# Decoder layer on one core: probabilities turned by TensorE instead of by DMA, routing moved to GpSimd, keys quantised in PSUM

## What is computed

```python
x = x + attn(layernorm(x))                 # each token's 16 heads against each other's channels, RoPE
x = x + cross(layernorm(x), ctx)           # 16 heads of 16, 2048 queries x 2048 keys
x = x + moe(layernorm(x))                  # 8 experts, top 2, and a shared expert
# cross: q, k rounded to 127 levels per head and token, v per channel,
#   p = softmax(q k^T);  s = max(p)/255;  p = round(p/s)*s;  out = (p v) Wp + bp
# moe:   g = sigmoid(x Wg); the two largest of g + bias keep g, the others get 0
#   out = sum_e silu((g_e x) w1_e) * ((g_e x) w3_e) @ w2_e + shared(x)
```

## Time and profile before

| | |
|---|---|
| median of 3 runs (range) | 1097.98 us (1095.16 to 1098.07) |
| profiled execution, its own time | 1099.65 us |
| span of the profiled execution | 1097.9 us |
| granted PE clock, mean | 0.899 of full |
| busy: PE, DVE, ACT, POOL | 71%, 88%, 70%, 64% of the span |
| DMA queue of SP | 76% of the 16 engines' span |
| first `keep_scores` starts | at 115.82 us |
| last exponential ends | at about 1062.1 us |

### The profile page before, as it was taken

The page is one execution under the profiler, slowest core; times in us unless marked ns, Lnnn a source line. Parts: engine busy times, 40 slices in busy tenths (PEclk is TensorE's granted clock), DMA queues, the critical chain, the costliest instruction groups (busy, mean ns, idle before and its releaser), DMA issues. The chain is left out here.

```text
span 1097.9 us, 21898 instructions
## 1 busy us (share of the span) xinstructions
PE 777.0 (71%) x7206; PEld 463.3 (42%) x7328; DVE 967.4 (88%) x1907; ACT 768.0 (70%) x1019; POOL 704.1 (64%) x776
## 2 busy tenths in 40 slices
PE   6766655767686867777686858686767867776764
PEld 4434333444343534444344534443434444444443
DVE  4895888999999999999998999999999999898952
ACT  2434666688777777776868877777778686878762
POOL 6445886867676768768686768686776858620101
PEclk9876688989999999889998999899899889899986
DMA  6011478979796979798896969697979789699970
GB/s 220 1 39 43 84 136 143 167 123 166 129 161 123 172 121 172 128 140 159 137 180 116 169 116 173 120 178 121 164 134 154 145 136 178 118 160 148 172 130 5
DMA packets 540887, 147.71 MB, mean 135 GB/s; under 512 B 534115, under 2 KB 538726, under 8 KB 540390
## 3 DMA queue, kind: packets, MB, share of 16 engines
q1 hardware_dynamic: 540774, 146.31, 76.0%
HBM read 9.96 MB, written 2.10 MB: 11 GB/s over the span
## 5 line engine op out<-in xcount | busy, mean ns | idle before, releaser
L1066 DVE TENSOR_SCALAR_CACHE_REDUCE score<-ps_score,q_neg 128x1024 f32<-128x1024 f32 x512 | 636.7, 1276 | 39.9 <-PE ps_score L1408 38.2
L757 ACT ACTIVATE prob<-score,exp_bias 128x2048 uint16<-128x2048 f32 x256 | 511.6, 1999 | 50.9 <-DVE exp_bias L1076 50.5
L1408 PE MATMUL ps_score<-keys,queries 128*128 128x512 bf16 x902 | 304.6, 413 | 135.3 <-DVE score L1066 116.7
L1426 PE MATMUL ps_pv<-prob_t,values 128*32 128x128 f16 x4096 | 152.0, 233 | 53.6 <-DMA prob_t<-prob 53.3
L508 POOL TENSOR_TENSOR product<-hs_exp,v_tok 128x1024 f32<-128x1024 f32 x64 | 149.1, 2353 | 47.7 <-ACT hs_exp L725 47.7
L1426 PEld LDWEIGHTS ps_pv<-prob_t,values 128*32 128x32 f16 x4096 | 128.8, 103 | 115.0 <-issue 115.0
L518 POOL TENSOR_TENSOR folded<-product 128x512 f32<-128x512 f32 x128 | 165.5, 1315 | 10.7 <-DVE hs L1003 7.0
L1408 PEld LDWEIGHTS ps_score<-keys,queries 128*128 128x128 bf16 x1024 | 70.2, 101 | 237.4 <-DVE score L1066 195.7
L508 POOL TENSOR_TENSOR product<-qk_rot 128x1024 f32<-128x1024 f32 x64 | 149.4, 2357 | 4.0 <-POOL qk_rot L501 4.0
L799 ACT ACTIVATE routed_both<-normed,routed_gate 128x256 bf16<-128x256 f32 x124 | 52.7, 496 | 94.2 <-POOL routed_gate L484 94.2
L1280 PE MATMUL ps<-routed_both,w 128*128 128x128 bf16 x512 | 47.2, 248 | 17.8 <-ACT routed_both L806 16.9
(11 more groups left out here) (133 smaller groups left out, 1225.9 us busy)
## 6 DMA issues: line engine op xcount, KB each, us to landing
prob_t<-prob SPq DMA_TRANSPOSE x256, 4.5
prob_t<-in_w SPq DMA_DIRECT2D x3, 1024.0 KB, 5.0
x_in<-in_x SPq DMA_DIRECT2D x16, 128.0 KB, 3.3
score<-in_cond_t SPq DMA_DIRECT2D x4, 512.0 KB, 6.9
out<-x_out SPq DMA_DIRECT2D x16, 128.0 KB, 2.5
w_qkv<-in_w_qkv SPq DMA_DIRECT2D x1, 768.0 KB, 4.3
early<-in_w_kv SPq DMA_DIRECT2D x1, 512.0 KB
w_s<-in_w_s SPq DMA_DIRECT2D x3, 128.0 KB
```

The lines of the kernel that those rows point to most:

```text
L757: act.activation(prob[:, s, :].bitcast(U16), score[:, s, :], ACT.Exp, bias=exp_bias[:, s:s + 1], scale=-1.0, accum_out=prob_sum[:, t.par, ...
L1066: dve.tensor_scalar(score[:, s, HALF * i:HALF * i + HALF], ps_score[:, i].rearrange("p b k -> p (b k)"), q_neg[:, t.par, h:h + 1], None, A ...
L1408: mm = pe.matmul(ps_score[:, i, b, :], queries[:, t.par, h // 2, h % 2, :], keys[:, h // 2, k0:k0 + KEYS], start=True, stop=True)
L1426: mm = pe.matmul(out[j], beside_zeros(values, i, h + j), prob_t[:, (h + j) % RING, i, :], start=(i == 0 and first), stop=(i == T - 1 and l ...
```

## The change

- The turning of the probabilities goes from the DMA to PE: `turn(h)` makes 16 transposes into a slot of `ps_score`, two substeps after the head's scores (`TURN = 2`), and a 128x1024 copy as int32 (`keep_turned`) brings them to SBUF. ACT makes 12 of a tile's 16 copies, DVE the four at substeps 11 to 14.
- The two slots of `ps_score` now serve three users in a fixed round: half 0, half 1, the turned probabilities of head `h-2`.
- The sigmoid moves from DVE to POOL (`choose` has 13 operations, one of them a power). PE spreads the gates along the partitions (`spread_gates`, 4 fp32 matmuls of 128 columns, twice), ACT keeps them (`keep_gates`, 128x512, twice), and POOL multiplies the tokens that are already turned by them (`route`, 128x1024, twice), ahead of `shift_scores`. ACT's `route` and `keep_routed` and PE's `routed_turn` are gone.
- POOL folds the value products once more (4 `fold_more` of 128x256 a tile), and DVE reduces two halves at once: 2 + 2 reductions of 512 numbers a tile in place of 4 of 256 and 4 of 512.
- Two of the small results of the query rounding stay in PSUM and one operation goes.
- Keys: all intermediate results stay in PSUM, in three banks by turns; values use one bank. The first two tiles' own values and projection use other banks, and the order of the first stage is changed to fit (queries of the first tile are turned after two of the four value turns; `cast_experts(1)` comes after the queries).
- Last tile: DVE chooses the experts (`choose_last`, 7 operations with a sort of 8) and multiplies by the gates straight from PSUM (`route_last`), and `experts_out` begins after four experts.

```diff
-                        sp.dma_start_transpose(prob_t[:, h % RING], prob[:, h % RING, :]
-                                               ).then_inc(prob_turned[h % RING], 16)
...
+TURN = 2
+DVE_KEEPS = (11, 12, 13, 14)
+        def key_bank(u):
+            return ps_score[:, u % 3 // 2, u % 3 % 2, :]
+        def slot(h, i):
+            return (h + i) % 2
...
             def scores(h, i, t):
-                if (due := t.due(2 * H, 2 * h + i - 1)) is not None:
+                if (due := t.due(2 * H, 2 * h + (0 if i == 0 else -1))) is not None:
                     pe.wait_ge(score_kept, due)
+                if i == 1 and (due := t.due(H, h - TURN)) is not None:
+                    pe.wait_ge(turn_kept, due)
...
-                    mm = pe.matmul(ps_score[:, i, b, :], queries[:, t.par, h // 2, h % 2, :],
+                    mm = pe.matmul(ps_score[:, slot(h, i), b, :], queries[:, t.par, h // 2, h % 2, :],
...
+            def turn(h, t):
+                pe.wait_ge(prob_ready, t.count(H, h + 1))
+                pe.wait_ge(score_kept, min(t.count(2 * H, 2 * (h + TURN) + 1), T * 2 * H))
+                if (due := t.due(H, h - 1)) is not None:
+                    pe.wait_ge(turn_kept, due)
+                out = ps_score[:, slot(h + TURN, 2)].rearrange("p b k -> p (b k)").bitcast(F16)
+                for i in range(T):
+                    mm = pe.transpose(out[:, P * i:P * i + P], prob[:, h % RING, P * i:P * i + P], ident_f16[:])
+                mm.then_inc(turn_made, 1)
...
+            def keep_turned(h, t):                       # ACT; DVE has the same with tensor_copy
+                act.wait_ge(turn_made, t.count(H, h + 1))
...
+                act.copy(prob_t[:, h % RING].rearrange("p k q -> p (k q)").bitcast(I32),
+                         ps_score[:, slot(h + TURN, 2)].rearrange("p b k -> p (b k)").bitcast(I32)
+                         ).then_inc(turn_kept, 1)
...
+            def route(i, t):                             # POOL
+                pool.wait_ge(gate_kept, t.count(2, i + 1))
...
+                pool.tensor_tensor(routed_t[:, EG * i:EG * i + EG],
+                                   normed_t[:, 2].unsqueeze(1).to_broadcast([P, EG, C, P]),
+                                   gate_wide[:, EG * i:EG * i + EG, :].unsqueeze(2).to_broadcast([P, EG, C, P]),
+                                   ALU.mult).then_inc(routed_kept, 1)
...
                     if n.exists() and h == 13 + late:
                         keep_queries(n)
+                    if m.exists() and t.exists() and h in (13, 14):
+                        keep_gates(h - 13, m)
                     if a.exists() and h == 14:
                         head_exp(a)
+                    if h >= TURN and t.exists() and h not in DVE_KEEPS:
+                        keep_turned(h - TURN, t)
...
-                dve.tensor_tensor(k_int[:], kp, over(k_inv[:], HD), ALU.mult).then_inc(k_chain, 1)
+                dve.tensor_tensor(kp, kp, over(k_inv[:], HD), ALU.mult).then_inc(k_chain, 1)
```

More of the change, by code:

```diff
@@ L230, in layer_kernel @@
         bank = {n: ctx.enter_context(nc.psum_tensor(f"ps_{n}", [P, 512], F32)) for n in (5, 6, 7)}
+        q_max = bank[5][:, 0:H]
+        q_float = heads(bank[6][:, D:2 * D])
+        k_max = bank[7][:, 0:2 * H]
         bank_bf = {n: bank[n][:, :].bitcast(BF16) for n in bank}
@@ L262, in layer_kernel @@
         prob_ready = sem("prob_ready")
-        prob_turned = [sem(f"prob_turned{i}") for i in range(RING)]
+        turn_made = sem("turn_made")
+        turn_kept = sem("turn_kept")
         pv_done = sem("pv_done")
@@ L586, in body @@
                     fold_more(3, a)
+                if m.exists() and t.exists():
+                    route(0, m)
+                    route(1, m)
                 if a.exists():
@@ L607, in _ @@
             all_scores(first)
+            ln_scale(0, second)
             shift_scores(first)
@@ L612, in _ @@
             fold(G + 1, first)
-            ln_scale(0, second)
+            fold_more(G, first)
+            fold_more(G + 1, first)
             value_products(2, first)
@@ L617, in _ @@
             fold(G + 3, first)
+            fold_more(G + 2, first)
+            fold_more(G + 3, first)
             norm_ho(first)
[L620 to L621 removed]
             rope(second)
@@ L630, in _ @@
             fold(G + 1, second)
+            fold_more(G, second)
+            fold_more(G + 1, second)
             over_tiles(body)
@@ L771, in keep_one @@
                     act.wait_ge(xo_projected, due)
-                act.copy(x_one[:, t.par, :], bank[7][:, 0:D]).then_inc(one_done, 1)
+                act.copy(x_one[:, t.par, :], one_bank(t)[:, 0:D]).then_inc(one_done, 1)
             def keep_two(t):
@@ L1045, in quantise_queries @@
+                dve.wait_ge(q_chain, t.count(5, 2))
+                dve.reciprocal(q_inv[:], q_neg[:, t.par, :]).then_inc(q_chain, 1)
+                dve.wait_ge(q_chain, t.count(5, 3))
+                dve.scalar_tensor_tensor(out=q_float, in0=heads(bank[6][:, 0:D]), scalar=-HD ** -0.5,
                                          in1=over(q_inv[:], HD), op0=ALU.mult, op1=ALU.mult).then_inc(q_chain, 1)
-                dve.wait_ge(q_chain, t.count(6, 5))
+                dve.wait_ge(q_chain, t.count(5, 4))
@@ L1470, in routed_turn @@
                 for e in range(EG):
-                    for c in range(C):
-                        j = C * e + c
-                        mm = pe.transpose(bank_bf[6 + i][:, P * j:P * j + P],
-                                          routed[:, EG * i + e, P * c:P * c + P], ident_bf[:])
-                mm.then_inc(routed_turned, 1)
+                    mm = pe.matmul(bank[6 + i][:, P * e:P * e + P], routed_gate[:, EG * i + e:EG * i + e + 1]
+                                   .to_broadcast([P, P]), ident[:], start=True, stop=True)
+                mm.then_inc(gate_spread, 1)
             def experts(i, j, t):
```

413 lines of the change are left out of this document (220 added, 193 removed).

## The result

The changed kernel takes 1221.32 us (median of 4 runs, 1220.84 to 1221.92) where the kernel before, on the same chip, takes 1097.05 (1095.16 to 1098.07). The ratio is 1.1135, with a 95% interval of 1.1116 to 1.1154: 124 us slower. The forecast was 1167, in a range of 1065 to 1205. The direction was right, the size was not, and the time is almost that of rival C, 1225. Whether it is C's mechanism as well is what most of the experiments ask.

What follows compares the result with a forecast made beforehand. The prediction took DVE, 88% busy, to set the tiles. From a span of 1097.9 us, +105 for the tiles, -28 for the first stage and -8 for the tail gave 1166.9, or 1167 on the runs' scale; range 1065 to 1205.

Steps and rivals of the forecast that it cites:

- rival C: In the tiles, all of ACT's turned copies come late behind waits: 69 us a tile, 1225 us; chance 0.11.
- 15 tiles +105: All tiles: a period of 65.2 us, +7.0 each, counted 15 times, adds 105 us.
- DVE's own work, +0.9: DVE in each tile: four added PSUM copies (+4.8) less removed operations, net +0.9 us, bounds 0 and +1.5.
- The slots, +3.4 (1.5 to 4): Score slots: half 0 waits for DVE's copy of the previous head's half 1, +3.4 us a tile, mostly in light heads.
- PE, +0.8 (0 to 2): PE in each tile: with the transposes, lists of heads 3, 6 and 7 end late, +0.8 us.
- ACT, +3.2 (0.5 to 8): ACT in each tile: turned copies stand behind waits and delay PE's half 1 and DVE, +3.2 us.
- -1.3 gained: In each tile, PE's waits for a DMA and some of ACT's go: -1.3 us, bounds 0 and 2.
- First stage, -28: Ahead of the tiles: products in PSUM speed the key steps (-20), the stage's end gains more; -28 us, bounds -15 and -34.
- Tail, -8: Behind the last exponential: faster turn, expert choice, gates and earlier output product; -8 us, bounds -5 and -11.
- B: In the tiles, DVE stays the bound: +0.8 us a tile, 1075 us (1055 to 1093); chance 0.27.
- D: Whole kernel: all cancels at 2.4 us a tile, 1095 to 1101 us; chance 0.05.
- E: In the tiles, PE's clock falls and transposes slow down: 71 us a tile, 1255 us; chance 0.05.

Runs made afterwards that it cites:

- e10: Second folding of the value products taken off GpSimd, against the changed kernel with the turning back on the DMA (1057.6 us): 1048.75 us.
- e12: Only the keys' intermediates kept in PSUM, k_max left in SBUF, against the kernel before: 12.2 us less.

## Why the forecast was off, step by step

**Where it stands in pieces.** The forecast's span was 1166.9, the measured one 1219.2: 52.3 too few. Of these 27.2 are the period (15 x 1.81), 16.4 the stretch from the first score copy to the first xo_t, 5.4 the first stage (-22.6 for -28) and 3.3 the tail.

**The first step that failed: "15 tiles +105".** I took the period from the earlier trace rows and multiplied by the 15 between its marks. The stretch ahead of the first mark, 80.3 us, has a whole tile and five heads of the next, each with the same copies and slots, and no term. It grew by 16.4 us. The turning does it: 81.9 us without it, 96.7 with it. That is 31% of the miss, and plain arithmetic. The other step is the next one.

**The second, and the larger: DVE's own work, +0.9**, which was two numbers of different kinds in one. The copies (+4.8) measured 2.6, with ACT's already short. What was taken off DVE (-3.9) measured -1.3 without the turning and -0.3 with it, together with all else of the change. This is where the period's 1.8 went: 3.6 too few here, less the 1.8 by which the turning alone came in under its terms. I let removed work count in full in a kernel whose DVE I had just said would wait for PE; DVE now waits 140 us for scores, and less work between such waits mostly lengthens them. That is the reading that fits, not one that an experiment isolates. Without the turning a part goes to GpSimd's longer list, as the 0.46 us of e10 show; the rest wasn't taken apart.

**The slots, +3.4 (1.5 to 4)**: 2.6 to 3.0 alone. Right, by the right mechanism.

**PE, +0.8 (0 to 2)**: not settled. Leaving the transposes out brought nothing in two experiments, but in both the clock fell, and by the score matmuls alone that can hide 2 to 3 us a tile. The term was formed at an unchanged clock, and the clock rose. PE's busy time in the tiles, put at 59 us, reads 52 (626.0 us in the 800 from 200 to 1000; the trace lacks some of its score matmuls).

**ACT, +3.2 (0.5 to 8)**: the copies' length is worth 3.7. Not comparable item by item: xo_raw, which I had at 1.0 to 1.7, measured 1.45. For head_exp the forecast was right that hs_max comes as late as `route`, and wrong to price it by the one copy behind it: it waits 3.5 us a tile (5.4 us in the whole run before), and moving it doesn't help, since it lies on a ring.

**The turning in sum**: my terms for it make 4.8 + 3.4 + 0.8 + 3.2 - 1.3 = 10.9 us a tile; measured are 10.07 with the rest and 9.13 alone. So the sum was sized well, and the miss is elsewhere. Its terms were not all so: DVE's copies measured about half, and PE's term and the "-1.3 gained" have no clean measurement. That they come out right together is partly luck.

**First stage, -28.** The keys alone gave 15.0 for -20, with k_max in SBUF; the whole change 22.6. The steps came to 6.37 us for 6.0, 2.6 us in seven. In e12 k_scale took up to 1.87 us and ended with GpSimd's product, while k_max, with its input in PSUM, stayed at 0.68 us beside the same product (28.23 to 28.91). The Trainium skill, "SBUF — State Buffer", section "SBUF: two separate sides", speaks of an exclusive lock between VectorE and GpSimd, held for a whole instruction. These rows agree with it and speak against mere crowding of the memory. k_scale has only one input in SBUF, so by that page it would have to run in a two-port mode, which no row shows.

**Tail, -8**: -6.0 from the last exponential, -4.7 from the last xo_t. The choice itself is as short as forecast (1.4 us). Without the turning the tail gains 2.6 where 5.3 were forecast; which wait behind the gates takes the rest was not taken apart.

**The rivals.** B (DVE stays the bound) is refuted: DVE waits 140 us. C gave the time, and part of its mechanism: 69 us was too much for the mean period (66.98), and it had put all of it on waits ahead of ACT's copies, where putting the copies first gives back 0.8. Its time came out right by luck: its 3.8 us a tile over A happen to be near the whole miss of 52.3 us, 3.5 a tile, of which the period has only 1.8. D is out. E is refuted, and its opposite seen: the clock rose, and sixteen transposes take 1.06 us at a granted 1.00, the pace of the eight in 0.62. The Trainium skill, "TensorE: Matmul & The Clock Gate", section "Part 4: PE-mode transpose", reports that the full clock doesn't engage for transposes. Here it does, and the measurement decides.

**The signs.** The period (66.98, in 63 to 67) and DVE's wait for scores (140 us, over 100) came as the forecast said; the steps (6.37 us for 6), the first score copy (93.2 for 88) and PE's busy time did not. The mechanism in the slots was right, and the time still missed by the two steps above.

**What stays open.** Of the 3.8 us that bare turning costs, 0.8 to 1.2 have no experiment of their own, nor has the "-1.3 gained". The clock's part in the two kernels with one transpose wasn't taken apart from PE's, so the transposes' own cost stays open, between nothing and some 3 us a tile.

## What to carry to other kernels

Before moving a transfer's work to the engines, ask what buffer its result goes through: here the turned tile took a third share in two PSUM slots, and that order alone cost 2.6 to 3.0 us a tile, and made copies out of the slot, on an engine with 27% to spare, links of the chain. Count a removed operation only where its engine is still the bound after the change: 3.9 us off DVE brought 0.3 here. Look at the granted clock before reading what leaving work out of TensorE brings. And a per-period term has to be multiplied by all the work that carries it, not by the gaps between the marks that measured it.

## What the runs showed of the hardware that I had not expected

- A 128x32 operation of VectorE with input and output in SBUF took up to 1.87 us (2.28 in the kernel before, row below) when a GpSimd product ran, and 0.19 in all eight cases with its input in PSUM.
- TensorE with more to do was granted the higher clock: 0.899 over the span before, 0.974 with the transposes, 0.88 with one in sixteen of them; in the stretch from 400 to 460 us 0.89, 1.00 and 0.94.
- GpSimd's power of 128x8 numbers takes 1.68 us, that of 128x1 0.60: from these two sizes, some 0.15 us for each number ((1677 - 604) / 7 ns, an estimate).

```profile
L912 DVE TENSOR_SCALAR k_scale<-k_max x8: 181/182/2279, 18.2 to 80.1; 128x32 f32<-128x32 f32 x8
```
```profile
L413 POOL TENSOR_TENSOR rstd<-var_eps,minus_half 128x1 f32<-128x1 f32 x48 | 29.0, 604 | 8.8 <-POOL var_eps L409 8.8
...
L462 POOL TENSOR_TENSOR gate<-gate_exp,minus_one 128x8 f32<-128x8 f32 x15 | 25.2, 1677 | 2.7 <-POOL gate_exp L459 2.7
```
